# Candidate banks by direction, the projection in the reset bank, and the order selection in ten-token pieces, in a bidirectional GRU kernel

## What is computed

```python
xn = layernorm(x) * gamma + beta
# gradients of the gray image -> small MLP -> softmax -> argmax: idx, one number per image
seq_h = xn.reshape(B, 1024, C)
seq_v = swapaxes(xn, 1, 2).reshape(B, 1024, C)
seq = where(idx == 1, seq_v, seq_h)          # the order selection
z = seq @ in_w.T + in_b
yf = gru(z @ wih_f.T + bih_f, whh_f, bhh_f, reverse=False)
yb = gru(z @ wih_b.T + bih_b, whh_b, bhh_b, reverse=True)
out = x + concat(yf, yb) @ out_w.T + out_b

def step(h, xt):                              # 1024 of them, one after the other
    (hr, hz, hn), (xr, xz, xn) = split(h @ whh.T + bhh), split(xt)
    r, z = sigmoid(xr + hr), sigmoid(xz + hz)
    n = tanh(xn + r * hn)
    return (1 - z) * n + z * h
```

## Time and profile before

| what | value |
|---|---|
| time, median of 3 runs | 1733.62 us (1731.27 to 1734.33) |
| the profiled execution, its own time | 1740.94 us |
| its span | 1739.1 us |
| TensorE busy | 1622.2 us (93%), 21570 matmuls |
| VectorE busy | 1496.9 us (86%) |
| ScalarE busy | 1191.5 us (69%) |
| DMA traffic | 31.04 MB, mean 18 GB/s |

### The profile page before, as it was taken

The page is one execution under the profiler, slowest core; times in us unless marked ns, Lnnn a source line. Parts: engine busy times, 40 slices in busy tenths (PEclk is TensorE's granted clock), DMA queues, the critical chain, the costliest instruction groups (busy, mean ns, idle before and its releaser), DMA issues.

```text
span 1739.1 us, 61541 instructions
## 1 busy us (share of the span) xinstructions
PE 1622.2 (93%) x21570; PEld 1287.0 (74%) x21570; DVE 1496.9 (86%) x9055; ACT 1191.5 (69%) x6271; POOL 57.1 (3%) x126
## 2 busy tenths in 40 slices
PE   3547999999999999999999999999999999999997
PEld 2435777777777777777777777777777777777776
DVE  7879888888888888888888888888888888888887
ACT  6735667777677776767667777677767677677766
POOL 5520000000000000000000000000000000000000
PEclk9755555555555555555555555555555555555555
DMA  5200000000000000000000000000000000000000
GB/s 159 80 7 8 12 14 11 15 11 14 12 14 12 12 13 11 14 12 15 11 14 7 13 13 13 11 14 11 15 11 15 11 14 12 13 13 13 13 13 16
DMA packets 40102, 31.04 MB, mean 18 GB/s; under 512 B 3448, under 2 KB 37624, under 8 KB 39800
## 3 DMA queue, kind: packets, MB, share of 16 engines
q1 hardware_dynamic: 39800, 27.13, 5.4%
HBM read 18.73 MB, written 8.39 MB: 16 GB/s over the span
## 4 chain that ended last, share of the span: by engine, by line
DVE 69%; ACT 21%; issue 8%; PE 1%; DMA 0%; POOL 0%; SPq 0%; DVEq 0%; ACTq 0%; POOLq 0%
DVE state L895 30%; ACT drive L498 21%; DVE bank L884 18%; DVE halves L904 12%; DVE big L876 4%; DVE seq L860 1%; DVE stats L732 1%; DVE weighted L758 1%; DMA gamma_row<-in_gamma 0%; DVE moments L737 0%; PE bank L541 0%; PE bank L545 0%; PE bank L594 0%; POOL xin L363 0%; PE bank L528 0%
## 5 line engine op out<-in xcount | busy, mean ns | idle before, releaser
L594 PEld LDWEIGHTS bank<-halves,wsplit 128*128 128x128 f16 x18432 | 726.9, 107 | 348.3 <-DVE halves L904 257.9
L594 PE MATMUL bank<-halves,wsplit 128*128 128x16 f16 x18432 | 901.7, 182 | 47.6 <-DVE halves L904 44.6
L895 DVE TENSOR_TENSOR_SCAN state<-gain,drive 128x48 f32<-128x48 f32 x2048 | 526.9, 257 | 175.3
L594 PE MATMUL bank<-seq,wcomb 128*128 128x128 f32 x1536 | 592.9, 482 | 0.2 <-DVE seq L860 0.2
L492 ACT ACTIVATE rpair<-bank 128x16 f32<-128x16 f32 x2048 | 379.4, 185 | 246.3 <-PE bank L594 246.3
L498 ACT ACTIVATE drive<-bank 128x16 f32<-128x16 f32 x2048 | 395.2, 193 | 220.5 <-DVE bank L884 16.4
L884 DVE TENSOR_TENSOR_SCAN bank<-rpair,bank 128x32 f32<-128x32 f32 x2048 | 459.3, 224 | 3.4 <-ACT rpair L492 3.4
L904 DVE SCALAR_TENSOR_TENSOR halves<-state 128x32 f16<-128x32 f32 x2048 | 398.7, 195 | 35.5
L495 ACT ACTIVATE gain<-bank 128x16 f32<-128x16 f32 x2048 | 393.0, 192 | 31.6
L594 PEld LDWEIGHTS bank<-seq,wcomb 128*128 128x128 f32 x1536 | 385.9, 312 | 0.7 <-DVE seq L860 0.7
L911 DVE SCALAR_TENSOR_TENSOR drive<-gain,state 128x16 f32<-128x16 f32 x2046 | 365.6, 179 | 0.0
(11 more groups left out here) (115 smaller groups left out, 203.1 us busy)
## 6 DMA issues: line engine op xcount, KB each, us to landing
xin<-in_x SPq DMA_DIRECT2D x16, 512.0 KB, 3.5
big<-in_x SPq DMA_DIRECT2D x124, 64.0 KB
out<-big SPq DMA_DIRECT2D x124, 64.0 KB
wih<-in_wiht SPq DMA_DIRECT2D x2, 384.0 KB
con<-in_consts SPq DMA_DIRECT2D x1, 424.0 KB, 5.0
whh<-in_whht SPq DMA_DIRECT2D x2, 192.0 KB
xin<-in_x SPq DMA_DIRECT2D x4, 64.0 KB
out<-xin SPq DMA_DIRECT2D x4, 64.0 KB
```

The costliest lines, as they stand in the source:

```text
L594: return nc.tensor.matmul(o, w, m, start=start, stop=True, skip_group_check=True)
L895: v.tensor_tensor_scan(state[:, d, ring, :], gain[:, e, cols], drive[:, e, cols], 0.0, ALU.mult, ALU.subtract).then_inc(state_ready[d], 1)
```

## The change

- There are four NX banks, one for each q and direction. A direction's candidate goes to the upper half of its own NX bank, so that the scan reads and writes one bank. TensorE's wait on the other direction's candidate scan is gone. Each NX bank is opened by its own first bias matmul.
- `Y` is the upper half of the reset bank that is being filled for the next block, whose first bias matmul opens it ahead of the projection.
- `EDGE` is 16 tokens. The other 992 tokens are selected over the first 16 blocks, in the six steps of each that have no `add_output`, in pieces of 10, 10 and 11 tokens from either end: 96 pieces of 160 or 176 elements per partition, in the same place between `hold_state` and `new_state` of direction 0.
- The residual tiles of the first and the last 16 blocks lie in `xin`. SyncE waits for `select_rest` only ahead of tile 16, TensorE not at all.

```diff
 TPP = L // P
-EDGE = 4 * TB
+EDGE = 2 * TB
+EARLY = 16
-    R, Z, NX, Y = bank[0:2], bank[2:4], bank[4:6], bank[6]
-    cand = bank[7]
+    R, Z = bank[0:2], bank[2:4]
+    NX = (bank[4:6], bank[6:8])
+    Y = [R[q][:, 2 * P:4 * P] for q in range(2)]
+
+    def candidate_of(q, e, d):
+        return NX[q][d][:, 2 * P + 2 * B * e:2 * P + 2 * B * (e + 1)]
...
+    def tile_of(k):
+
+        early = k if k < EARLY else k - (NBLK - 2 * EARLY)
+        return xin[:, early // TPP, early % TPP, :] if min(k, NBLK - 1 - k) < EARLY else tiles[:, k, :]
...
-        sp.wait_ge(select_rest, 1)
         for i in range(1, NBLK // 4):
             for q in range(2):
+                if i * 2 + q == EARLY:
+                    sp.wait_ge(select_rest, 1)
                 load_tiles(i * 2 + q, q, i * 4 + (2 * q - 2))
...
-                                   cand[:, (2 * e + d) * 2 * B:(2 * e + d + 1) * 2 * B].rearrange("p (n k) -> p n k", k=2)[:, :, 1],
+                                   candidate_of(q, e, d).rearrange("p (n k) -> p n k", k=2)[:, :, 1],
...
-        def nx(q):
-            return NX[q][:, :].rearrange("p (s d b k) -> p s d b k", s=TB, d=2, k=2)
+        def nx(q, d):
+            return NX[q][d][:, 0:2 * P].rearrange("p (s b k) -> p s b k", s=TB, k=2)
...
             k = 0 if which == G_HN else 1
-            return mm(nx(q)[:, :, d, :, k], bias6[:, which * HID:(which + 1) * HID],
+            return mm(nx(q, d)[:, :, :, k], bias6[:, which * HID:(which + 1) * HID],
                       ind[:, :].rearrange("p (s d b) -> p s d b", s=TB, d=2)[:, :, d, :],
-                      start=(which == G_HN and d == 0))
...
-                return mm(nx(q)[:, :, d, :, 1], w, src)
+                return mm(nx(q, d)[:, :, :, 1], w, src)
...
-        def project(q, d):
+        def project(q, d, start=False):
             h = state[:, d, q * TB:(q + 1) * TB, :].rearrange("p s (b k) -> p (s b) k", k=3)[:, :, 1]
-            return mm(Y[:, d * C:(d + 1) * C], h, outw[:, d, :], start=(d == 0))
-
-        def output_bias():
-            return mm(Y[:, 0:C], ones3[:, :], obias[:, :])
+            return mm(Y[q][:, d * C:(d + 1) * C], h, outw[:, d, :], start=start)
+
+        def output_bias(q):
+            return mm(Y[q][:, 0:C], ones3[:, :], obias[:, :])
...
-            out_of = {G_R: gate(R, q)[:, at, d, :], G_Z: gate(Z, q)[:, at, d, :], G_N: nx(q)[:, at, d, :, 0]}
+            out_of = {G_R: gate(R, q)[:, at, d, :], G_Z: gate(Z, q)[:, at, d, :], G_N: nx(q, d)[:, at, :, 0]}
...
             parts = ((0, high), (1, high), (2, low))
             run(G_R, parts).then_inc(reset_pre[d], 1)
-            if not alone:
-                pe.wait_ge(cand_pre[o], others)
             run(G_N, parts).then_inc(reset_and_hn[d], 1)
             if not alone:
                 pe.wait_ge(update_ready[o], others)
...
-                    output_bias().then_inc(y_ready, 1)
+                    output_bias(1 - q).then_inc(y_ready, 1)
...
-                    project(1 - q, 0)
+                    project(1 - q, 0, start=not filling)
...
-        body(0, 0)
-        pe.wait_ge(select_rest, 1)
-        for i in range(1, L // RING - 1):
+        for i in range(L // RING - 1):
             body(i * RING, i * 2)
...
-        project(1, 0)
+        project(1, 0, start=True)
         project(1, 1)
-        output_bias().then_inc(y_ready, 1)
+        output_bias(1).then_inc(y_ready, 1)
...
-            v.tensor_tensor(t, Y[:, d * C:(d + 1) * C], t, ALU.add).then_inc(y_used, 1)
+            v.tensor_tensor(t, Y[j % 2][:, d * C:(d + 1) * C], t, ALU.add).then_inc(y_used, 1)
...
-            at = (place(s, d) * 2 + d) * 2 * B
+            at = place(s, d) * 2 * B
             dve.wait_ge(reset_and_hn[d], 2 * turn)
-            v.tensor_tensor_scan(cand[:, (2 * e + d) * 2 * B:(2 * e + d + 1) * 2 * B],
-                                 rpair[:, e, 2 * B * d:2 * B * (d + 1)], NX[q][:, at:at + 2 * B], 0.0,
+            v.tensor_tensor_scan(candidate_of(q, e, d),
+                                 rpair[:, e, 2 * B * d:2 * B * (d + 1)], NX[q][d][:, at:at + 2 * B], 0.0,
                                  ALU.mult, ALU.add).then_inc(cand_pre[d], 1)
...
-        def body(base, kblk, first):
-            share = (L - 2 * EDGE) // RING
+        SELECT_AT = (0, 1, 2, 3, 4, 6)
+        SHARE = (0, 10, 20, 31)
+
+        def select_piece(kblk, n):
+
+            side, third = n % 2, n // 2
+            t0, t1 = (EDGE + kblk * SHARE[-1] + SHARE[third + k] for k in range(2))
+            return select(t0, t1) if side == 0 else select(L - t1, L - t0)
+
+        def body(base, kblk):
             for r in range(RING):
                 q, s = r // TB, r % TB
                 candidate(base, r, 0)
@@ -920,9 +930,9 @@
                     hold_state(base, r, 0)
                 if s in (5, 7) and kblk + q > 0:
                     add_output(kblk + q - 1, (s - 5) // 2)
-                if first:
-                    ins = select(EDGE + r * share, EDGE + (r + 1) * share)
-                    if r == RING - 1:
+                if kblk + q < EARLY and s in SELECT_AT:
+                    ins = select_piece(kblk + q, SELECT_AT.index(s))
+                    if kblk + q == EARLY - 1 and s == SELECT_AT[-1]:
                         ins.then_inc(select_rest, 1)
                 new_state(base, r, 0)
...
-            body(i * RING, i * 2, i == 0)
+            body(i * RING, i * 2)
```

More of the change, by code:

```diff
@@ L242, in build @@
     tile_in = (tile_in0, tile_in1)
-    def tile_of(k):
-        early = (0, 1, NBLK - 2, NBLK - 1)
-        return xin[:, 0, early.index(k), :] if k in early else tiles[:, k, :]
     x_tok = x.rearrange("b h w c -> b (h w) c")
@@ L609, in fill_bias_half @@
             k = 0 if which == G_HN else 1
-            return mm(nx(q)[:, :, d, :, k], bias6[:, which * HID:(which + 1) * HID],
+            return mm(nx(q, d)[:, :, :, k], bias6[:, which * HID:(which + 1) * HID],
                       ind[:, :].rearrange("p (s d b) -> p s d b", s=TB, d=2)[:, :, d, :],
-                      start=(which == G_HN and d == 0))
+                      start=(which == G_HN))
         def fill_input(q, kblk, g, d):
```

## The result

After: 1706.4 us, the median of six runs (1705.61 to 1707.31); before beside it 1734.0 us (1731.27 to 1738.99). The ratio is 0.984, with an interval of 0.9823 to 0.9852: faster by 27.6 us, against the 33.2 us forecast (1700.4 us, with a range of 1693 to 1710 for the forecast itself). The executions that were profiled, 1740.9 us before and 1707.3 us after, are 33.6 us apart; the forecast for the profiled one was 1707.7 us.

The account below looks back on a forecast made before the run. Two loops bound the step: VectorE and ScalarE need 1.540 us, TensorE's queue adds 0.024. 14.2 + 0.6 + 18.4 - 0 = 33.2 us off 1733.6 gives 1700.4 us; forecast's own range 1693 to 1710, overall 1693 to 1722.

Parts of the forecast that it names:

- The selection, 14.2 us: First ring's 16 steps: what 16 selection pieces of 1.23 us on VectorE add, 14.2 us, goes away.
- The edge pieces, 0.6 us: At the start, two pieces of 256 elements replace two of 0.698 us: 0.6 us less, bound below 0.
- A piece's duration, 0.28 us: New selection pieces on VectorE: 0.28 us for 160 elements, 0.30 for 176; all 96 cost 0 to 1 us.
- The wait, 1.56 to 1.52 us in TensorE's loop: Removing direction 1's wait on direction 0's candidate scan shortens TensorE's loop from 1.56 to about 1.52 us.
- The steady step, 0.018 us × 1022 = 18.4 us: Each recurrence step becomes 0.018 us shorter, period 1.546 us: 18.4 us in all, bounds 0 and 24.5.
- The 0.12 us between direction 1's halves and direction 0's scan: VectorE's spacing would have to be 0.10 us at period 1.540; no gain if 0.12 is the floor.
- Cost of one bank for the scan, 0: Candidate scan reading and writing one bank: taken as 0, upper bound 0.066 us per scan.
- From the sum to the median: Profiled execution forecast at 1707.7 us; median taken 7.3 us below it, 1700.4 us.
- 1 (VectorE's order keeps 1.564): VectorE's order takes the wait's place, period stays 1.564, only the selection gains: 1719 us; chance 0.14.
- 2: One bank for the scan's read and write costs time: 1734 us (chance 0.05) or 1768 us (chance 0.05).
- 3 (pieces cost 0.14 each): Selection pieces on VectorE don't overlap: 0.14 x 96 = 13 us, giving 1714 us; chance 0.05.
- 4 (clock rises): A denser TensorE queue holds the 2.4 GHz clock: 20 us more gain, 1680 us; chance 0.03.

Follow-up runs that it names:

- e2_selection_only: The kernel before with only the new selection (16 edge tokens, 96 pieces over 16 blocks), banks and waits as before: 1719.0 us, ratio 0.991.
- e6_even_moving: The kernel after with the moving operand of the four half bias matmuls in its own contiguous tile: 1703.4 us, ratio 0.980.
- e8_aligned_pieces: The kernel after with selection pieces of 12, 12 and 8 tokens, cut at multiples of four tokens: 1704.7 us, ratio 0.981.
- e1: The kernel after with TensorE's wait on the other direction's candidate scan put back, nothing else: 1719.7 us, ratio 0.991.
- before: The unchanged kernel before, its first profiled execution: 1740.9 us.
- before_again: The unchanged kernel before, executed once more for a second profile: 1737.0 us.

## Why the prediction was right, point by point

**The selection, 14.2 us.** Right, and for its reason: the first ring is shorter by 39.24 − 24.90 = 14.3 us (0.3 us of it are the shorter steps, less what the pieces cost), and the selection alone (`e2_selection_only`) makes the kernel faster by 14.5 us.

**The edge pieces, 0.6 us.** 437 ns and not 390 for each of two, against 710: 0.5 us. No run tells it apart.

**A piece's duration, 0.28 us.** Wrong, 0.39 us. The prediction drew a line through elements, from two lengths whose lines and elements rise together, and applied it to pieces that aren't cut at lines. The cost of 0 to 1 us for all of them was nearly right nevertheless: the first 128 steps took 199.1 us, 1.555 us each, against 1.546 later, which is 1.2 us for 96 pieces (0.8 and 1.1 us in the two other executions). The state scan starts 0.25 to 0.29 us after a piece, longer before its end than the 0.10 us that the prediction took from the earlier trace rows.

**The wait, 1.56 to 1.52 us in TensorE's loop.** Right in each part: the group of direction 1 takes 0.41 us, putting the wait back restores the 0.46 and the period, and TensorE has room for one small matmul and not for three.

**The steady step, 0.018 us × 1022 = 18.4 us.** Right in the profiled pair, 1.564 to 1.546 us. Over all profiled executions of the two kernels it is a little less: before 1.564 and 1.562, mean 1.563; after 1.546, 1.552 and 1.548, mean 1.549. That makes 0.0146 × 1007 = 15 us (0.0146 from the unrounded periods). With the runs that have the same steady steps (`e2_selection_only` with those before, `e6_even_moving` and `e8_aligned_pieces` with those after) it is 0.0165 × 1007 = 17 us. So this term was too large by 1 to 3 us, and periods differ by up to 0.006 us within one kernel, which one profile did not show.

**The 0.12 us between direction 1's halves and direction 0's scan.** Here the prediction reasoned wrongly, without harm to its number. It read one pair, had the spacing shrink towards 0.10 us, and said that nothing would come if 0.12 were the floor. By the averages above it was 0.129 us before and is 0.118 after, and it went below 0.116 in no run: 0.12 is near enough the floor, and the gain came all the same. The leg from direction 0's halves to its sigmoid fell from 0.553 to 0.534 us, and its scan comes only 0.010 us later behind the sigmoid. The choice of 0.018 between bounds of 0 and 0.024 was not much more than a guess, and it came true in this pair.

**Cost of one bank for the scan, 0.** Right: 222 ns against 224, and e1 equals e2 in time.

**From the sum to the median.** The prediction took the profiled execution as 7.3 us above the median before and carried that over. It isn't carried over: the profiled execution after is 0.9 us above its median. So the forecast met the profiled execution, 1707.7 against 1707.3 us, and missed the median by 6 us. Even the first was in part luck: the recurrence of that execution starts 1.9 us sooner than the one before (115.9 against 117.7), where the prediction had 0.6. With the mean periods the sum is 14.3 + 0.5 + 15 − 1 = 29 us; the medians show 27.6 in one comparison and 32.3 in the other. The gain is so known to some 5 us, too little to settle a term of 3 us.

The instant of the first sigmoid forms two groups: 115.9 to 117.7 us in `before`, `before_again`, `e2_selection_only` and the profiled kernel after, 110.2 to 112.9 us in the other ten. In the traces they part at about 50 us, in the folding of the weights, at instructions that the change leaves alone. Time lines of TensorE in the kernel after and in `e1_wait_back`:

```profile
49.53 2.91 PE L547 MATMUL bank<-wih,inw 128*128 128x384 f32 x4
...
48.24 1.54 PE L547 MATMUL bank<-wih,inw 128*128 128x384 f32 x4
```

The same four matmuls take 2.91 us in one and 1.54 in the other, and so it is in all executions of the two groups. The profile gives a granted clock of 1.00 there in both, so it doesn't show the cause. Three of three profiles with the old banks are in the late group and one of eleven with the new; whether that is chance isn't known, and for the executions that weren't profiled the start isn't either.

**The rivals.** 1 (VectorE's order keeps 1.564): no, the period is 1.546 to 1.552, though its premise, that 0.12 can't shrink, is nearly true. 2: no, scans of 222 ns. 3 (pieces cost 0.14 each): no, 1.2 us / 96 = 0.012. 4 (clock rises): no. The granted clock stays at 0.50, the 1.2 GHz level, with TensorE busy 24.39 of the second ring's 24.89 us:

```profile
140.76:165.65 24.89, 24.39 (x340) 18.32 (x335) 23.37 (x145) 17.11 (x97) 0.00 (x0) 0.50 0.05 13
```

The Trainium skill ("TensorE: Matmul & The Clock Gate", section "Part 1: The HAM clock gate") has activity lift the throttle. Here TensorE was 98% busy with small matmuls and the rows keep it at half speed.

## What to carry to other kernels

When the chain of waits names VectorE and an engine at 93% has 1% of it, look for a stretch of the same kernel with all waits and less work on that engine: here the last block, 1.540 against 1.564 us, gave an upper bound of the gain beforehand. Work that is off the path can be moved into a place that an engine must idle in anyway, but the place's width, 0.23 us here, is to be compared with how soon the next instruction can follow, not with the duration. And sums for a median should be made with more than one profiled execution: one alone was 7 us off, a quarter of the gain.

## What the runs showed of the hardware that was not expected

- The predicated copy goes by the 16-byte lines that its rows touch: 224, 298, 373 and 436 ns for one to four lines on each of 16 rows, whatever part of the last line is used.
- A bias operand from SBUF makes a 16-column activation from PSUM 82 to 91 ns longer (185 to 274, 192 to 274, 192 to 283 ns).
- A bf16 bias matmul of 128 columns into every second column of a bank lasts 390 ns, that of 256 columns 389 ns, with a moving operand with or without gaps. The output bias, 128 columns too, but contiguous and with three rows, takes 283 ns. (The ends of matmuls are modelled.)
- The distance of the two directions, in the steps with a gate bias matmul, hardly moves within an execution (0.660 us in two of the kernel after, 0.667 in a third) and differs between them, and the period goes from 1.546 to 1.552 us.
- The same four matmuls of the first stage take 1.54 us in ten executions and 2.91 in four, at a granted clock of 1.00 in the profile of both, and the recurrence starts some 4 us later in the four.
